# Token MLP, minGRU and routed experts in one kernel: four places for routed results, final stores from two engines, statistics and logits copies at other spots

## The reference

```python
h = gelu_tanh(codebook[x] @ W1 + b1) @ W2 + b2             # 256 -> 1024 -> 256
s = layernorm(h)
for l in (0, 1):                                           # minGRU, two layers
    k, v = s @ Wz[l].T + bz[l], s @ Wh[l].T + bh[l]
    s = scan over time of  s_t = sigmoid(-k) * s_{t-1} + sigmoid(k) * g(v)
h = h + s
n = layernorm(h)
shared = (gelu(n @ w1s) * (n @ w2s)) @ w3s                 # 256 -> 1024 -> 256
e = argmax(n @ Wg)                                         # one of 8 experts for each token
routed = (gelu(n @ E1[e]) * (n @ E2[e])) @ E3[e]
return h + shared + routed
```

## Time and profile before

| what | value |
|---|---|
| median of 3 runs (lowest, highest) | 489.27 us (489.18, 489.71) |
| the profiled execution itself | 489.65 us |
| span of its profile | 487.9 us |
| granted TensorE clock | 1.000 |
| busy: PE, PE weight load | 98%, 88% |
| busy: DVE, ACT, POOL | 68%, 51%, 17% |
| chain that ended last | PE 81%, DVE 10%, ACT 3%, issue 3% |
| 40 slices, PE | 8 in the first, 5 in the last, 9 elsewhere |

### The profile page before, as it was taken

One profiled execution on the slowest core, in us unless ns is written; L12 is line 12 of the kernel. 1 busy time (PEld: TensorE's weight loads), 2 busy tenths in 40 slices (PEclk: granted clock), 3 DMA queues, 4 the chain that ended last, 5 costly groups with the idle time before them and its releaser, 6 DMA issues.

```text
span 487.9 us, 8515 instructions
## 1 busy us (share of the span) xinstructions
PE 477.8 (98%) x3052; PEld 427.0 (88%) x3053; DVE 330.0 (68%) x540; ACT 247.0 (51%) x376; POOL 82.7 (17%) x92
## 2 busy tenths in 40 slices
PE   8999999999999999999999999999999999999995
PEld 7898888888888887888788999799999998999885
DVE  3559678578686868868645587646785776777463
ACT  3767774575653463443334556336545473555321
POOL 5431031011011001102460002100200021020351
PEclk9999999999999999999999999999999999999999
DMA  5942121001210002200444455505553356250372
GB/s 156 378 129 85 34 75 55 32 23 48 66 62 1 1 0 93 83 0 23 151 145 79 171 171 201 194 24 182 187 196 145 134 199 215 97 194 14 113 270 93
DMA packets 25543, 55.12 MB, mean 113 GB/s; under 512 B 7264, under 2 KB 18784, under 8 KB 21536
## 3 DMA queue, kind: packets, MB, share of 16 engines
q1 hardware_dynamic: 19472, 43.58, 26.5%
q0 software_dynamic: 2976, 8.14, 4.9%
q10 hardware_dynamic: 3056, 2.88, 2.0%
HBM read 42.25 MB, written 12.35 MB: 112 GB/s over the span
## 4 chain that ended last, share of the span: by engine, by line
PE 81%; DVE 10%; ACT 3%; issue 3%; DMA 1%; POOL 1%; another core or an unknown queue 1%; DVEq 0%; POOLq 0%
PE ps L278 22%; PE ps L279 21%; PE ps L280 21%; PE ps L791 6%; PE ps L793 3%; PE ps L821 2%; DVE hT L1213 1%; DVE w_slots L1241 1%; DVE ps L1219 1%; DVE stats L1278 1%; DMA q<-codebook_in,idx_sb 1%; PE ps L605 1%; PE ps L823 1%; PE ps L640 1%; ACT hT L966 1%
## 5 line engine op out<-in xcount | busy, mean ns | idle before, releaser
L278 PE MATMUL ps<-xW,w_slots 128*128 128x256 f32 x256 | 73.6, 287 | 0.1
L280 PE MATMUL ps<-xW,w_slots 128*128 128x256 f32 x256 | 72.4, 283 | 0.0
L279 PE MATMUL ps<-xW,w_slots 128*128 128x256 f32 x256 | 72.4, 283 | 0.0
L1213 DVE TENSOR_TENSOR hT<-ps,hT 128x512 fp32r<-128x512 f32 x64 | 43.9, 686 | 36.6 <-ACT hT L955 17.1
L476 POOL DMA_INDIRECT y_tokens<-y_rows,row_ids x30 | 36.1, 1203 | 188.1 <-DVE y_rows L1595 169.6
L1575 DVE TENSOR_TENSOR w_slots<-stage,w_slots 128x2048 fp32r<-128x2048 f32 x24 | 54.8, 2285 | 3.3 <-ACT w_slots L1103 2.7
L278 PEld LDWEIGHTS ps<-xW,w_slots 128*128 128x128 f32 x256 | 48.7, 190 | 0.9 <-DVE xW L1347 0.3
L279 PEld LDWEIGHTS ps<-xW,w_slots 128*128 128x128 f32 x256 | 48.8, 191 | 0.0
L280 PEld LDWEIGHTS ps<-xW,w_slots 128*128 128x128 f32 x256 | 48.7, 190 | 0.0
L966 ACT ACTIVATE hT<-ps 128x512 fp32r<-128x512 f32 x32 | 19.1, 597 | 54.6 <-DVE ps L1219 53.0
L791 PE MATMUL ps<-w_slots,hW 128*128 128x512 f32 x128 | 46.6, 401 | 0.0
(11 more groups left out here) (208 smaller groups left out, 1277.1 us busy)
## 6 DMA issues: line engine op xcount, KB each, us to landing
stage<-ew_in SPq DMA_DIRECT2D x24, 1024.0 KB, 4.8
x_sorted<-zero_row SPq DMA_DIRECT2D x16, 128.5 KB
x_sorted<-zero_odd SPq DMA_DIRECT2D x16, 128.5 KB
stage<-w1s_in SPq DMA_DIRECT2D x2, 1024.0 KB, 7.8
fetched<-y_tokens SPq DMA_DIRECT2D x4, 512.0 KB, 5.6
x_pair<-x_sorted ACTq DMA_DIRECT2D x7, 256.0 KB, 2.8
out_rows<-fetched SPq DMA_DIRECT2D x3, 512.0 KB, 3.0
first_stage<-tok_w_in SPq DMA_DIRECT2D x1, 1024.0 KB
```

The costliest lines, as they stand in the source:

```text
L278: pe.matmul(dst, lhs_hi, rhs_hi, start=start, stop=False, skip_group_check=shares_bank)
L279: pe.matmul(dst, lhs_hi, rhs_lo, start=False, stop=False, skip_group_check=shares_bank)
L280: return pe.matmul(dst, lhs_lo, rhs_hi, start=False, stop=stop, skip_group_check=shares_bank)
L1213: dve.tensor_tensor(hT[:, c % RING, 1, :], ps[:, bank, :], f32(hT[:, c % RING, 0, :]), ALU.subtract).then_inc(h_lo, 1)
```

## The change

- **Places.** `WAYS = 4` places in `y_rows` instead of two, and four semaphores `y_stored`. POOL issues scatter i and then waits for i - 3, so three are on their way. `y_rows` and `xTp` exchange their regions of SBUF.
- **Unread rows.** All of `x_sorted` is filled with `zero_row`, the row numbers are floats, and `y_tokens` has four tiles of rows behind the tokens instead of two. A DVE function `spread_unread` in the opening expert adds 128 times (tile number mod 4) to the numbers that are no tokens and writes them as integers to `to_rows`, which POOL's scatters use. POOL waits for it instead of for the load.
- **Final stores.** Of the last four, SP issues tiles 0 and 2, ACT tiles 1 and 3.
- **Other spots on DVE.** `unit_value` is cut in two: L1312 becomes `unit_product`. It stays right behind the first half but for unit 7 (chunk 25), where it comes with the late scan in chunk 26, and unit 15, where `copy_logits(1)` goes between them. Statistics and moments of block 2 (second norm) go from chunk 38 to chunk 36, in front of unit 13's value.
- **Weights.** Piece 3 is split in chunk 11 instead of 9, on ACT and DVE.

```diff
-    SPLIT_PIECES = {7: (0,), 8: (1, 2), 9: (3,), 11: (4,), 12: (5,), ...
+    SPLIT_PIECES = {7: (0,), 8: (1, 2), 11: (3, 4), 12: (5,), ...
-    y_tokens = nc.dram_tensor("y_tokens", [(TILES + 2) * P, D], F32, kind="Internal").ap()
+    y_tokens = nc.dram_tensor("y_tokens", [(TILES + WAYS) * P, D], F32, kind="Internal").ap()
-        y_rows = at("y_rows", [P, 2 * D], F32, r_xl + 2 * K)
+        y_rows = at("y_rows", [P, WAYS * D], F32, r_ring + 24 * K)
-        xTp = at("xTp", [P, 2, KD, P], F32R, r_ring + 24 * K)
+        xTp = at("xTp", [P, 2, KD, P], F32R, r_xl + 2 * K)
...
@@ block.sync
-                sp.dma_start(x_sorted[j * P:(j + 1) * P, :], (zero_row, zero_odd)[j % 2][:]).then_inc(zeroed, 16)
+                sp.dma_start(x_sorted[j * P:(j + 1) * P, :], zero_row[:]).then_inc(zeroed, 16)
...
-            sp.wait_ge(y_stored[0], ((back + 1) >> 1) * 16)
-            sp.wait_ge(y_stored[1], (back >> 1) * 16)
+            for p in range(WAYS):
+                sp.wait_ge(y_stored[p], ((back + (WAYS - 1 - p)) >> 2) * 16)
...
-            for i in range(BT):
+            for i in range(0, BT, 2):
                 t = (BLOCKS - 1) * BT + i
                 sp.wait_ge(summed, BLOCKS + i)
                 sp.dma_start(out_v[:, t, :], fetched[:, t, :]).then_inc(out_stored, 16)
@@ block.gpsimd
-            pool.sem_inc(y_free, 2)
+            pool.sem_inc(y_free, WAYS)
...
+            pool.iota(unread_by[:], [[0, 2 * WAYS], [P, WAYS]], base=0, channel_multiplier=0,
                       allow_small_or_imprecise_dtypes=True).then_inc(pool_const, 1)
...
-            pool.wait_ge(ids_land, 16)
+            pool.wait_ge(ids_done, 1)
             for i in range(XT):
                 pool.wait_ge(y_taken, i + 2)
                 to_tokens(i)
-                if i:
-                    pool.wait_ge(y_stored[(i - 1) % 2], 16 * ((i - 1) // 2 + 1))
+                if i >= WAYS - 1:
+                    j = i - (WAYS - 1)
+                    pool.wait_ge(y_stored[j % WAYS], 16 * (j // WAYS + 1))
                     pool.sem_inc(y_free, 1)
-            pool.wait_ge(y_stored[(XT - 1) % 2], 16 * ((XT - 1) // 2 + 1))
+            for j in range(XT - (WAYS - 1), XT):
+                pool.wait_ge(y_stored[j % WAYS], 16 * (j // WAYS + 1))
@@ block.scalar, at its end
+            out_v = out.rearrange("(t p) d -> p t d", p=P)
+            for i in range(1, BT, 2):
+                t = (BLOCKS - 1) * BT + i
+                act.wait_ge(summed, BLOCKS + i)
+                act.dma_start(out_v[:, t, :], fetched[:, t, :]).then_inc(out_stored, 16)
@@ block.vector
                 dve.scalar_tensor_tensor(out=g, in0=ps[:, P_BANK, :], scalar=bh_twice[:, c:c + 1], in1=g, op0=ALU.add,
                                          op1=ALU.max).then_inc(m_done, 1)
+
+            def unit_product(u):
+                g = v_gate[:, u % 2, :]
                 dve.wait_ge(m_done, u + 1)
                 dve.scalar_tensor_tensor(out=g, in0=t_gate[:, u % 2, :], scalar=1.0, in1=g, op0=ALU.add,
                                          op1=ALU.mult).then_inc(v_done, 1)
...
             late_scan = {17: 3, 25: 7, 33: 11}
+            late_product = {25}
...
                 if c - 1 in late_scan and c < MLP:
+                    if c - 1 in late_product:
+                        unit_product(late_scan[c - 1])
                     unit_scan(late_scan[c - 1])
...
                 for u in UNIT.get(c, ()):
+                    if u == UNITS - KD - 1:
+                        row_stats(2, 2)
+                        row_moments(2, 2)
                     unit_value(u)
+                    if u == UNITS - 1:
+                        copy_logits(LOG_END[c])
+                    if c not in late_product:
+                        unit_product(u)
                     if c not in late_scan:
                         unit_scan(u)
...
-                if c in LOG_END:
-                    copy_logits(LOG_END[c])
-                if c == 38:
-                    row_stats(2, 2)
-                    row_moments(2, 2)
...
-                dve.tensor_reduce(y_rows[:, bass.ds(((done + 1) & 1) * D, D)], ps[:, bank, :].rearrange("p (h n) -> p n h", h=2), AX,
+                dve.tensor_reduce(y_rows[:, bass.ds(((done + (WAYS - 1)) & (WAYS - 1)) * D, D)], ps[:, bank, :].rearrange("p (h n) -> p n h", h=2), AX,
                                   ALU.add).then_inc(y_taken, count)
+
+            def spread_unread():
+                dve.wait_ge(ids_land, 16)
+                dve.scalar_tensor_tensor(out=unread[:], in0=row_ids[:], scalar=float(TILES * P), in1=unread_by[:, 0:XT],
+                                         op0=ALU.is_ge, op1=ALU.mult).then_inc(unread_done, 1)
+                dve.wait_ge(unread_done, 1)
+                dve.tensor_tensor(to_rows[:], row_ids[:], unread[:], ALU.add).then_inc(ids_done, 1)
...
                 if opening:
                     add_rows(BLOCKS - 2)
                     single_rows_lo(0)
+                    spread_unread()
```

More of the change, by code:

```diff
@@ L39, in build @@
     XT = 2 * EXPERTS + MORE
+    WAYS = 4
     SURE = TILES
@@ L217, in build @@
         turns = small("turns", [P, TOTAL + 1], U16)
-        r_one = place[0]
-        zero_odd = small("zero_odd", [P, D + 1])
-        x_one = at("x_one", [P, D], F32, r_one)
+        x_one = small("x_one", [P, D])
         singles = small("singles", [P, EXPERTS])
@@ L226, in build @@
         row_ids = small("row_ids", [P, XT])
+        unread = small("unread", [P, XT])
+        unread_by = small("unread_by", [P, 2 * WAYS * WAYS])
+        to_rows = small("to_rows", [P, XT], I32)
         ps = ctx.enter_context(nc.psum_tensor("ps", [P, 8, NB], F32))
@@ L248, in build @@
         q_land = [sem(f"q_land{b}") for b in range(1, BLOCKS)]
-        zeroed = sem("zeroed"); zero_id = sem("zero_id"); zero_set = sem("zero_set"); ids_set = sem("ids_set"); ids_land = sem("ids_land")
+        zeroed = sem("zeroed"); zero_id = sem("zero_id"); zero_set = sem("zero_set"); ids_set = sem("ids_set"); ids_land = sem("ids_land"); unread_done = sem("unread_done"); ids_done = sem("ids_done")
         pool_const = sem("pool_const"); dve_const = sem("dve_const");
@@ L268, in build @@
         gT_ps = sem("gT_ps"); gT_hi = sem("gT_hi"); gT_lo = sem("gT_lo")
-        tile_done = sem("tile_done"); y_taken = sem("y_taken"); y_stored = [sem(f"y_stored{p}") for p in range(2)]; y_free = sem("y_free")
+        tile_done = sem("tile_done"); y_taken = sem("y_taken"); y_stored = [sem(f"y_stored{p}") for p in range(WAYS)]; y_free = sem("y_free")
         fetch_land = [sem(f"fetch_land{b}") for b in range(BLOCKS)]
@@ L349, in _ @@
             sp.dma_start(share_third[:], w3s).then_inc(share_land[2], 16)
[L351 to L352 removed]
+            sp.wait_ge(zero_set, 1)
+            sp.wait_ge(zero_id, 1)
             for j in range(XT + 2):
                 sp.wait_ge(h_lo, HC + j * 3 // 4)
[L356 removed]
+                sp.dma_start(x_sorted[j * P:(j + 1) * P, :], zero_row[:]).then_inc(zeroed, 16)
             sp.wait_ge(split_lo, 1)
@@ L423, in _ @@
             gather(0)
-            pool.iota(zero_row[:, D:D + 1].bitcast(I32), [[0, 1]], base=TILES * P, channel_multiplier=1).then_inc(zero_id, 1)
-            pool.iota(zero_odd[:, D:D + 1].bitcast(I32), [[0, 1]], base=(TILES + 1) * P, channel_multiplier=1).then_inc(zero_id, 1)
+            pool.iota(zero_row[:, D:D + 1], [[0, 1]], base=TILES * P, channel_multiplier=1,
+                      allow_small_or_imprecise_dtypes=True).then_inc(zero_id, 1)
             pool.memset(mhalf[:], -0.5).then_inc(pool_const, 1)
@@ L462, in _ @@
             pool.wait_ge(zeroed, 16 * (XT + 2))
-            pool.iota(xn2[:, :, D].bitcast(I32), [[P, TILES]], base=0, channel_multiplier=1).then_inc(ids_set, 1)
+            pool.iota(xn2[:, :, D], [[P, TILES]], base=0, channel_multiplier=1,
+                      allow_small_or_imprecise_dtypes=True).then_inc(ids_set, 1)
             pool.wait_ge(placed, 1)
@@ L476, in to_tokens @@
                 pool.indirect_dma_start(
-                    out=y_tokens, out_offset=bass.IndirectOffsetOnAxis(ap=row_ids[:, i:i + 1].bitcast(I32), axis=0),
-                    in_=y_rows[:, i % 2 * D:(i % 2 + 1) * D], in_offset=None,
-                    bounds_check=(TILES + 2) * P - 1, oob_is_err=True).then_inc(y_stored[i % 2], 16)
-            pool.wait_ge(ids_land, 16)
+                    out=y_tokens, out_offset=bass.IndirectOffsetOnAxis(ap=to_rows[:, i:i + 1], axis=0),
+                    in_=y_rows[:, i % WAYS * D:(i % WAYS + 1) * D], in_offset=None,
+                    bounds_check=(TILES + WAYS) * P - 1, oob_is_err=True).then_inc(y_stored[i % WAYS], 16)
+            pool.wait_ge(ids_done, 1)
             for i in range(XT):
@@ L675, in rank_products @@
                 pe.wait_ge(onehot_done, 1)
-                pe.wait_ge(pool_const, 7)
+                pe.wait_ge(pool_const, 8)
                 oh = onehot[:].rearrange("p t e -> p (t e)")
@@ L1382, in choose_experts @@
```

(2 more changed lines are left out.)

4 lines of the change are left out of this document (2 added, 2 removed).

## The result

| | before | after |
|---|---|---|
| median, same chip, 6 runs each (lowest, highest) | 489.43 us (489.18, 489.71) | 484.71 us (484.32, 485.25) |
| profiled execution / its span | 489.65 / 487.9 us | 484.74 / 483.0 us |
| granted TensorE clock | 1.000 | 1.000 |

The ratio is 0.9903, 95% interval 0.9891 to 0.9916: 4.7 us faster. The forecast was 487.0 and the range began at 485.9. The direction was right, the gain twice the forecast.

What follows compares the result with a forecast made beforehand. PE was taken as the bound, busy 477.8 of 487.9 us. Gains of 0.46 + 0.33 + 1.15 + 0.30 = 2.24 us from a 489.27 median gave 487.0; range 485.9 to 488.6.

Steps and rivals of the forecast that it cites:

- The holes at 45, 113, 190 and 192 us: PE idle in chunks 9-12, 26, 38 and 39, waiting for DVE; moves close them, gaining 0.46, 0.33 and 1.15 us.
- Moved statistics and spread row numbers: DVE at chunk 36 and opening expert: cost taken as 0; without cover 0.2 and up to 0.7 us.
- The final stores: End of program: ScalarE taking sums 1 and 3 starts the last store near 483.5, gain 0.3 us.
- closing steps of 2.3 us follow: End of program: after the last store lands at 485.6, a further 2.3 us of closing steps.
- gain 0: Expert loop: four places for routed results release nobody on PE's path; gain 0, bounds 0.5 us either way.
- The term of the tail: Final sums and stores: 0.30 us gained by two issuing engines; 1.2 were the landing halved too.
- The hole at 243: PE idle 1.05 us before 243.33, behind a ScalarE pause; forecast to stay.
- More: Rival, 11%: the ScalarE pause shortens or falls beside other work, 1.05 and 0.15 of hole go too: 485.8 us.
- Part: Rival, 15%: the pair of holes at 190 us returns, its margin being 0.4: 488.2 us.
- Given back: Rival, 12%: the 1.94 won earlier is waited out at ScalarE's pause near 239 us; only the tail stays: 489.0.
- Slower: Rival, 6%: ScalarE's two pauses before the gelus at 239 and 256 us lengthen; doubled, 492.5 us.
- the ±0.5 for the places: Expert loop: bounds on the four places' effect, the size of PE's one wait of note, for xTp.

Runs made afterwards that it cites:

- stores_only: Kernel before with only the last four stores shared, SP tiles 0 and 2, ScalarE 1 and 3: 490.23 us, ratio 1.0001.
- base_again: Kernel before once more, unchanged, for a second profile: 490.8 us, ratio 0.9995.
- after_two_ways: Changed kernel with four places in memory, but two given out and POOL waiting for scatter i - 1: 487.92 us, ratio 0.9951 to the kernel before.
- order_only: Kernel before with only the weight piece, unit 7's product, the logits copy and block 2's statistics moved: 487.8 us, ratio 0.9948.
- base_late_load: Kernel before with only SP's load of ew3[1] delayed until the first window's low part is done: 487.8 us, ratio 0.9986.
- places_only: Kernel before with only four places, three scatters on their way and spread unread row numbers: 488.18 us, ratio 0.9969.
- after_again: Changed kernel once more, unchanged, in the second group of runs: 486.42 us, ratio 0.9925 to the kernel before.
- after_late_load: Changed kernel with SP's 1 MB load of ew3[1] delayed until the first window's low part: 484.77 us, ratio 0.9876; repeated: 483.65, 0.9898.
- third group: Later runs on one chip: base_late_load, the late-load versions and one with the logits copy moved back; kernel before 488.74 us.

## Why the prediction was right and wrong, point by point

**The holes at 45, 113, 190 and 192 us: right.** Terms 0.46, 0.33, 0.39 and 0.76; steps of the shift 0.46, 0.41, 0.40 and 0.81. The holes stand in all five traces without the order edits (0.46 to 0.48, 0.32 to 0.33, 0.39, 0.76 to 0.77) and in none of the eight with all of them. The reading that carried was of order and start times on DVE: what stands ahead of the operation that PE waits for, by its own duration. The statistics at 45 came 0.61 earlier (0.60 worked out), `take_rows` 0.73 (0.75).

**Moved statistics and spread row numbers: right at nothing.** The two added DVE operations take 0.18 and 0.19 and PE doesn't wait behind them.

**The final stores: the term was near, its place wrong.** SP is through 2.4 behind DVE's DRAIN with two queues, in each of the traces, and 2.8 to 2.9 with one: 0.4, where 0.30 was forecast. The Trainium skill (Trainium Kernel Development and Optimization, Key Constraints) says that several issuers save only issue time; the landings agree, 1.8 with one queue and 1.7 and 1.8 with two. But the 0.4 counts only once POOL is out of the way, and stores_only gave 0.

**The step that failed: "closing steps of 2.3 us follow", and with it the "gain 0" of the four places.** I took the time behind the last landing as fixed. It is not: in the earlier trace rows the last store has landed at 485.6, and of the 2.3 to the end 2.0 is SP waiting for POOL. The argument for the places asked whom DVE's wait releases on PE's path, and its answer, nobody, was right for PE. But it took for granted that four places end the wait, and they don't: the four waits of 2.0 us are still there. And it never asked what POOL itself delays at the end. The closing DRAINs by line and the last rows of POOL, both in the trace of before, show it: last scatter at 479.99, then a DRAIN of 5.14 up to 487.7, and the end at 487.9. The term of the tail would have been the drain's excess: 2.0 by the trace, plus 0.4 for the stores behind it, once three scatters are on their way, and not 0.30; 2.3 was measured.

The profiles taken together, in us. "Lost" is from SP's DRAIN to the last event, less the 0.1 that it takes without a wait, from times rounded to 0.1:

| kernel | scatters on their way | POOL DRAIN starts, against DVE's | POOL DRAIN's end | end of the span | lost |
|---|---|---|---|---|---|
| before | 2 | -0.4 | 487.7 | 487.9 | 2.0 |
| stores_only | 2 | -0.5 | 488.2 | 488.4 | 2.3 |
| base_again | 2 | +1.0 | 490.2 | 490.4 | 3.4 |
| after_two_ways | 2 | -0.4 | 485.9 | 486.1 | 2.4 |
| order_only | 2 | -2.3 | 484.8 | 485.0 | 0.1 |
| base_late_load | 2 | -2.3 | 484.7 | 484.9 | 0.0 |
| places_only | 3 | -8.5 | 480.3 | 486.6 | 0 |
| after | 3 | -8.5 | 477.0 | 483.0 | 0 |
| after_again | 3 | -8.5 | 478.9 | 484.9 | 0 |

With three on their way POOL's DRAIN starts 8.5 us ahead of DVE's in all eight such traces: no tie, nothing lost. With two it is between 2.3 ahead and 1.0 behind, and what it costs varies from 0 to 3.4 between executions. That fits the 1.5 us of places_only by its ratio [0.2 to 2.8], against 2.0 in the one pair of profiles. It is not all of the spread: with three on their way single runs still took 492.93 (places_only) and 489.23 (after_again), and no trace was kept of one. What sets how far POOL lags with two on their way stays open. Two against three on their way is worth about 1.3 us by the ratios of after_two_ways and after_again, which are from different groups and have intervals that overlap; the mechanism rests on the traces, not on this difference.

**The hole at 243: I built on one trace.** I counted as part of the kernel and gave its going 11% ("More"). It went, by 1.31, and the hole at 268 came, by 1.52. The prediction said that new waits of PE in the opening expert, or another size of the hole at 243, would show it wrong; both came, though neither is the change's. Of the fourteen traces, five have both pauses of ScalarE, four have the second alone (a hole of 0.6) and five have none; base_again and after_again differ from their first traces in this. So the 485.8 of that rival was not reached by its mechanism. The two changes nearly cancel. The gain in the span, 4.9 where 2.24 was forecast, exceeds it by 2.6: 2.0 by the tail, 0.65 by the start, 0.1 each by the four holes and the small ones, less 0.2 for these two. Start and last term differ between executions of one kernel; the tail's 2.0 is the change's doing, though the table above shows that this, too, varies with the execution.

**The rivals.** "Part" and "Given back" fell: all four holes closed, and what was won ahead of 240 us stayed won. "Slower" fell: in no trace was a pause of ScalarE longer than 2.93. None of the rivals had a term for POOL at the end, so the range could not hold the time: the ±0.5 for the places came from the size of a wait of PE, in another stage.

**The better version.** after_late_load ran 1.65 below the kernel after on one chip, and is the fastest design here: 484.77 against 490.79 of before. In the third group it gave 483.65, and one run of a version without the late load 485.24. Its gain over the kernel after is shown on that one chip only: the kernel after was not run in the third group, where the ratio of 0.9898 is no better than the 0.9903 of the first pair.

## What to carry to other kernels

A program ends when its last engine ends: before taking the time behind the last store as fixed, list each engine's last instruction with its closing DRAIN, and ask which one the end waits for; work whose result nobody reads can be the bound there. Before buffers are added for a wait, look at which event gives a buffer free: here it was the issue of the next scatter, and two more places left the waits at 2.0 us. To learn how far a hole is the kernel's, look at the same hole in a second execution, best on another chip, before it is counted or left out: four holes here were the same within 0.02 us in every trace, two others came and went at 0.6 to 2.4 us. When an operation is moved out from in front of the one that is waited for, its own duration is the gain, as long as the chain behind its new place has that much idle time: unit 7 had it, unit 3 did not.

## What the runs showed of the hardware

- POOL's closing DRAIN took 5137 ns in all fourteen traces; DVE's took 461 or 464, ScalarE's 150 or 151 with stores at its end and 626 to 629 without.
- PE's COMPARE_BRANCH into the part with single tiles took 2.0 to 4.5 us in ten traces in which a 1 MB load was on its way beside it, and 0.80 to 1.00 in the four in which that load came later. It ended 2.4 to 2.6 us behind the start of a 16 KB packet of instruction queue q8 in all fourteen, and it is this packet that the load delayed. The length with the load varied in the same kernel: 2.02 and 3.52 before, 3.58 and 3.48 after, and the hole behind it was its length less 2.06 in all nine traces with a hole (0.70 behind 2.76, 2.40 behind 4.46), and none behind the 2.02.
- ScalarE paused 2.6 to 2.9 us near 237 or 254 us, and DVE 3.3 to 3.6 near 255, without a releaser in the trace, in nine traces of fourteen. No instruction packet was listed at these times. These are after_again's waits (engine, tile, line: us in total, times, longest):

```profile
ACT gelub L970 <- remote: 5.7, 2, 2.9
...
DVE ps L1231 <- remote: 3.5, 1, 3.5
```

What ends these pauses stays open, as does the start: the gathers of the codebook leave PE between 0 and 1 us of idle time, differently in each execution, and 0.65 of the 4.9 us of the first pair of traces is that.
